# A graph network's second layer: the first group of a round prepared ahead of the node chunk, an index copy behind it, and activation tables loaded ahead of waits

## What is computed

```python
# layer 0
h = x @ W;  e = leaky_relu(a_src[src] + a_dst[dst], 0.2)
alpha = softmax of e over the edges of one dst
x = layernorm(x + tanh(segment_sum(h[src] * alpha[:, None], dst) + bias))
# layer 1
h = gelu(x @ W_pre + b_pre)
aggr = segment_sum(h[src] * edge_attr, dst)
v = x + aggr
y = gelu(gelu(v @ W1 + b1) @ W2 + b2)
out = layernorm(x + (v + y))
```

## Time and profile before

| what | value |
|---|---|
| median of 3 runs | 3843.77 us (3841.44 to 6046.89) |
| the profiled execution, time | 3842.3 us |
| the profiled execution, span from first to last instruction | 3840.5 us |
| busy share of the span: PE, DVE, ACT, POOL | 64%, 64%, 33%, 73% |
| mean granted TensorE clock | 0.701 of full speed |
| PE clock by tenths of full speed, 40 slices | `7555555555555555555558999999999999989997` |
| the same for POOL's busy share | `7777777777777777777747777777776667667664` |

### The profile page before, as it was taken

How to read it: one execution, slowest core, us unless ns; L and a number is a source line. 1 busy time by engine, 2 the same in 40 slices (tenths; PEclk the granted TensorE clock), 3 DMA queues, 4 the chain that set the end, 5 groups by cost and what they waited for, 6 DMA issues and landing times.

```text
span 3840.5 us, 66559 instructions
## 1 busy us (share of the span) xinstructions
PE 2439.5 (64%) x16652; PEld 1975.8 (51%) x16653; DVE 2446.4 (64%) x6235; ACT 1261.5 (33%) x3762; POOL 2789.9 (73%) x2950
## 2 busy tenths in 40 slices
PE   5433343434344444444448998898898888888886
PEld 3333333333333333333336777676776676766665
DVE  7444444444566666666657777777777777777765
ACT  4433343434455555555542111111111111121112
POOL 7777777777777777777747777777776667667664
PEclk7555555555555555555558999999999999989997
DMA  5222222222222222222224344344343333334332
GB/s 97 43 42 42 42 43 42 43 42 43 44 43 43 43 43 42 45 43 43 45 49 113 88 97 94 90 94 93 88 92 87 87 88 87 86 82 91 86 83 58
DMA packets 351534, 254.21 MB, mean 66 GB/s; under 512 B 254081, under 2 KB 279122, under 8 KB 351291
## 3 DMA queue, kind: packets, MB, share of 16 engines
q0 software_dynamic: 94016, 146.16, 19.6%
q1 hardware_dynamic: 241880, 99.40, 11.2%
q10 hardware_dynamic: 15394, 6.42, 0.6%
HBM read 244.43 MB, written 7.25 MB: 66 GB/s over the span
## 4 chain that ended last, share of the span: by engine, by line
POOL 34%; PE 28%; issue 17%; DVE 9%; ACT 7%; ACTq 2%; DMA 1%; DVEq 1%; POOLq 0%; SPq 0%
POOL rows L654 34%; PE bank L960 20%; PE bank L947 5%; ACT onehot L706 3%; DVE hot L1311 2%; DVE node L1327 1%; DVE score L1210 1%; ACT pair L726 1%; PE bank L969 1%; ACTq L699 1%; DMA rows<-table,src_i 1%; PE bank L933 1%; ACT L793 1%; ACT L800 0%; DMA src_i<-in_src_dram 0%
## 5 line engine op out<-in xcount | busy, mean ns | idle before, releaser
L654 POOL DMA_INDIRECT rows<-table,src_i x2850 | 2697.6, 947 | 999.0 <-issue 863.3
L960 PE MATMUL bank<-node,hot 128*128 128x288 bf16 x9310 | 1255.2, 298 | 27.5 <-issue 16.3
L897 PE MATMUL bank<-onehot,rows 128*97 128x72 f32 (+1 forms) x3056 | 586.2, 369 | 813.0 <-ACT onehot L736 813.0
L960 PEld LDWEIGHTS bank<-node,hot 128*128 128x128 bf16 x9310 | 946.9, 103 | 297.0 <-issue 19.1
L1311 DVE TENSOR_SCALAR hot<-node,key 128x642 bf16<-128x642 int16 x1862 | 870.5, 538 | 271.7 <-PE bank L960 233.8
L897 PEld LDWEIGHTS bank<-onehot,rows 128*97 128x97 f32 x3056 | 532.1, 281 | 852.3 <-issue 787.4
L947 PE MATMUL bank<-onehot,rows 128*96 128x72 f32 (+1 forms) x3136 | 327.1, 266 | 132.6 <-DVE acc L1356 132.5
L947 PEld LDWEIGHTS bank<-onehot,rows 128*96 128x96 f32 x3136 | 314.8, 179 | 154.0 <-DVE acc L1356 119.8
L706 ACT ACTIVATE onehot<-iota,far_dst 128x72 f32 (+1 forms) x1568 | 385.3, 328 | 23.3 <-ACT far_dst L703 0.7
L1189 DVE SCALAR_TENSOR_TENSOR other<-onehot,bank 128x576 f32<-128x576 f32 (+1 forms) x196 | 121.9, 622 | 390.0 <-ACT bank L719 321.6
L806 ACT ACTIVATE pair<-dst_i 128x8 f32<-128x8 int32 x196 | 35.3, 180 | 983.2 <-DVE rows L1345 966.5
(11 more groups left out here) (171 smaller groups left out, 2010.9 us busy)
## 6 DMA issues: line engine op xcount, KB each, us to landing
attr<-in_edge_attr_dram SPq DMA_DIRECT2D x190, 336.0 KB
rows<-table,src_i POOLq DMA_INDIRECT x2850
node<-in_src_dram SPq DMA_DIRECT2D x195, 64.0 KB
attr<-in_edge_attr_dram SPq DMA_DIRECT2D x190, 48.0 KB
dst_i<-in_dst_dram SPq DMA_DIRECT2D x200, 4.0 KB
src_i<-in_src_dram SPq DMA_DIRECT2D x195, 4.0 KB, 2.3
src_i<-in_src_dram SPq DMA_DIRECT2D x190, 3.5 KB
dst_i<-in_dst_dram SPq DMA_DIRECT2D x190, 3.5 KB
```

The lines of the kernel that those rows point to most:

```text
L654: pool.indirect_dma_start(rows[:, u, j * width:(j + 1) * width], None, table, bass.IndirectOffsetOnAxis(ap=src_i[:, u, j:j + 1], axis=0))\
L897: last = pe.matmul(total[:, 0:w], rows0(u, it)[:, j, 0:D1], wide(weights, w)[:, j, :], start=j == 0, stop=j == TILES - 1)
L960: last = pe.matmul(p_got[t], hot[:, c % HOTS, i, t * P:(t + 1) * P], tab[:, a, :, :].rearrange("p k d -> p (k d)"), start=a == 0, stop=a = ...
```

## The change

In layer 1, on DVE, `message` of a round's fifth group now also makes the mask (`marked`) and the seven gathered tiles' products (`multiplied`) of the next round's first group, ahead of the chunk. In the first group itself `added` comes first, then the marks of piece 0, the first reduction, the product of the fetched tile, which raises `e1_msg`, and only then the other four reductions. On ACT `shorten_src` moves behind the chunk. PE starts a chunk on `f_var` of the chunk before, where it waited for DVE to arrive (`f_go`); ahead of the very last chunk it waits for the last addition. In both layers ACT runs a one-element activation of the function that comes next ahead of the wait, so that its table is loaded by then; after each round of layer 0 it does so for Exp.

```diff
+            def table_for(f, k):
+                act.activation(unused[:, k:k + 1], zeros[0:1, 0:1], f)
+
             def middle(c, blocks=MB):
+                table_for(ACT.Tanh, 0)
...
-            groups(act, weights, lambda it: due(act, it, middle), alone=2)
+
+            def middle_due(it):
+                due(act, it, middle)
+                table_for(ACT.Exp, 3)
+            groups(act, weights, middle_due, alone=2)
             rest(act, middle)
 
             def final(c, blocks=MB):
+                table_for(ACT.Gelu, 2)
...
+                table_for(ACT.Sqrt, 1)
                 act.wait_ge(f_st, 16 * (c + 1))
-                act.wait_ge(f_var, c + 1)
+                act.wait_ge(f_var, c + 2)
...
-                if u == SLOTS - 1 and fetching(it):
+
+            def final_due(it):
+                due(act, it, final)
+                if fetching(it):
                     shorten_src(it + 1)
...
             def final(c, blocks=MB):
-                pe.wait_ge(f_go, c + 1)
+                pe.wait_ge(f_var, c + 1)
...
+            def marked(g, it, u, lo, w):
+                v.wait_ge(e1_fed, g + 1)
+                v.tensor_tensor(wide(onehot[:, u, :], w), over_window(p_dst1, w),
+                                over_tiles(iota[:, bass.ds(lo, w)], w), ALU.is_equal).then_inc(e1_hot, 1)
+
+            def multiplied(it, u, tiles):
+                v.wait_ge(e1.rows[u], gathered1(it, u))
+                return v.tensor_tensor(rows[:, u, 0:tiles * D], rows[:, u, 0:tiles * D], p_attr[:, 0:tiles * D], ALU.mult)
+
+            def multiplied_fetched(it, u):
+                v.wait_ge(g_out, it * 2 + (u > 0))
+                at = slice((TILES - 1) * D, TILES * D)
+                return v.tensor_tensor(rows[:, u, at], got[:, u, :], p_attr[:, at], ALU.mult)
+
+            def added(g, prev, w):
+                v.wait_ge(e1.acc, g + 1)
+                here = bass.ds(prev, w)
+                v.tensor_tensor(acc[0:D, here], acc[0:D, here], p_acc1[:, 0:w], ALU.add).then_inc(e1.free, 1)
...
                 if booked(it, u) and u == 0:
+                    added(g, prev, w)
+                    if fetching(it):
+                        marks(it, 0)
                     taken(it, range(1))
-                    v.wait_ge(g_out, it * 2)
-                    v.tensor_tensor(rows[:, u, cut:TILES * D], got[:, u, :], p_attr[:, cut:TILES * D], ALU.mult)\
-                        .then_inc(e1_msg, 1)
+                    multiplied_fetched(it, u).then_inc(e1_msg, 1)
                     taken(it, range(1, BOOKED))
                 else:
-                    product.then_inc(e1_msg, 1)
-                v.wait_ge(e1.acc, g + 1)
-                here = bass.ds(prev, w)
-                v.tensor_tensor(acc[0:D, here], acc[0:D, here], p_acc1[:, 0:w], ALU.add).then_inc(e1.free, 1)
+                    marked(g, it, u, lo, w)
+                    if booked(it, u):
+                        multiplied_fetched(it, u)
+                    multiplied(it, u, TILES - booked(it, u)).then_inc(e1_msg, 1)
+                    added(g, prev, w)
...
+                if u == SLOTS - 1 and it is not ROUNDS - 1:
+                    next_reg = v.alloc_register("next_" + named(it, u, ws))
+                    v.reg_alu(next_reg, after, (1 << BITS) - 1, ALU.bitwise_and)
+                    marked(g + 1, it + 1, 0, v.snap(next_reg, min_val=0, max_val=N - 1), ws[1])
+                    multiplied(it + 1, 0, TILES - 1)
```

More of the change, by code:

```diff
@@ L261, in gnn @@
         m_v = sem("m_v")
-        f_go = sem("f_go")
         f_y1 = sem("f_y1")
@@ L834, in _ @@
             feed(0, 0, 0)
-            groups(act, ahead, lambda it: due(act, it, final), alone=1)
+            groups(act, ahead, final_due, alone=1)
             rest(act, final)
@@ L994, in _ @@
             groups(pe, gather_sum, alone=1)
+            pe.wait_ge(e1.free, GROUPS + SLOTS)
             rest(pe, final)
@@ L1301, in _ @@
             v.sem_inc(g_out, 1)
+            v.sem_inc(f_var, 1)
             v.tensor_copy(key[:, :], key_i[:, :])
@@ L1332, in message @@
                 lo, further, prev = window(u, "1_" + named(it, u, ws))
[L1333 to L1343, removed]
-                v.wait_ge(e1.rows[u], gathered1(it, u))
-                product = v.tensor_tensor(rows[:, u, 0:cut], rows[:, u, 0:cut], p_attr[:, 0:cut], ALU.mult)
                 if booked(it, u) and u == 0:
+                    added(g, prev, w)
+                    if fetching(it):
+                        marks(it, 0)
                     taken(it, range(1))
-                    v.wait_ge(g_out, it * 2)
-                    v.tensor_tensor(rows[:, u, cut:TILES * D], got[:, u, :], p_attr[:, cut:TILES * D], ALU.mult)\
-                        .then_inc(e1_msg, 1)
+                    multiplied_fetched(it, u).then_inc(e1_msg, 1)
                     taken(it, range(1, BOOKED))
                 else:
-                    product.then_inc(e1_msg, 1)
-                v.wait_ge(e1.acc, g + 1)
-                here = bass.ds(prev, w)
-                v.tensor_tensor(acc[0:D, here], acc[0:D, here], p_acc1[:, 0:w], ALU.add).then_inc(e1.free, 1)
+                    marked(g, it, u, lo, w)
[3 more added lines that the diff above has]
+                    added(g, prev, w)
                 after = None if g is LAST else load_window(g + 1)
@@ L1382, in final @@
                 st = Steps(v, f_v, c * 7, 7)
-                v.sem_inc(f_go, 1)
                 v.wait_ge(f_g2, c + 1)
```

1 line of the change is left out of this document (added).

## The result

The changed kernel takes 3743.92 us (median of 4 runs, 3742.97 to 3744.58) where the kernel before takes 3844.1, a ratio of 0.9741 (0.9722 to 0.9761). That is faster by 2.6%. The forecast was 3754.8 and the range 3745 to 3786, so the direction is right, but the forecast is 10.9 us too high and the time lies 1.1 us under the range. The profiled execution took 3744.58 us with a span of 3742.7, 97.8 less than before.

What follows compares the result with a forecast made beforehand. POOL was taken to bound the kernel until 2758 us in layer 1, PE and DVE after that; 3840.5 us of span less 87.7 of POOL idle time and 1.3 for the last chunk, plus 3.3, gave 3754.8 us, range 3745 to 3786.

Steps and rivals of the forecast that it cites:

- The bound: Layer 1: POOL sets the pace up to 2758 us, then PE and DVE (the consumer); gain capped at POOL's 87.7 us idle.
- The round without a chunk: Layer 1, head of round: PE's window sum starts 1.6 us earlier, fuller clock adds up to 2.7; 3.6 us gain taken.
- The round with a chunk: Layer 1: Gelu 2.3 us earlier, window sum 5.0 earlier, at most 8.1 with the clock; 6.5 us gain taken.
- Both together: Consumer's gain over 29 rounds of layer 1: 15 x 6.5 + 14 x 3.6 = 148 us, bounds 97 and 182.
- rival 3: Layer 1, ahead of the chunk: DVE's products wait for their gather, holding up the chunk; +33 us, about 3876; chance 0.03.
- Rival 4: POOL's gathers slow beside DVE's denser marks; 1% longer each would be 17 us, 3772 us; chance 0.03.
- Rivals 1 and 2: Layer 1: consumer still binds in part, 3784 us, chance 0.2; wait just moves to piece 0's fetch, about 3810, chance 0.06.
- the sum: Whole kernel: span 3840.5 - 87.7 - 1.3 = 3751.5 us, plus 3.3 to the median, giving 3754.8 us.
- 94.0 - 21 x 0.3 = 87.7 us is real idle time: POOL in late layer 1: 21 waits for `src_i`, 94.0 us, less an ordinary gap each, leave 87.7 us to win.
- Layer 0: Table loads ahead of waits lie behind POOL; only the last two chunks can show, -2.6 to +0.8 us, taken as 0.
- The median of the runs is 3.3 us above this profile's span: Whole kernel: 3.3 us added to the forecast span of 3751.5 us to get the forecast run time of 3754.8.
- The tail: Last chunk, after all gathers: saves one table load, 1.3 us.

Runs made afterwards that it cites:

- six_after_3: The changed kernel with POOL making six gathers per booked group of layer 1, not seven, so part of the messages is missing: 3645.35 us, ratio 0.9505.
- products_behind: The changed kernel with the next round's first-group products back behind the chunk, only the mask ahead: ratio 0.9548, on a chip where the kernel before takes 5675 to 5805 us.
- l0_tables_3: The kernel before with only layer 0's part of the change, the one-element ACT activations that load tables early: 3837.74 us, ratio 0.9986.
- l1_only_2: The kernel before with only layer 1's part, all of the change but layer 0's four activation lines: 3746.98 us, ratio 0.977.
- add_late_3: The changed kernel with the addition moved back behind the reductions, as it stood before: 3771.9 us, ratio 0.9835.

## Why the prediction was right, and where it was not

The mechanism was right, and the sizes that went into the last sum were not. The step that failed is "3840.5 - 87.7 - 1.3 = 3751.5 us of span" with 3.3 us put on top: POOL's idle time was 92.6 us and not 87.7 (layer 1 won 91.6), layer 0 was put at nothing and the span got 4.95 us shorter there, and 1.2 us and not 3.3 lie between the span and the median.

**The bound.** POOL's pace against the consumer's, the change of hands at 2758 us, and the cap at POOL's idle time all held: idle time went from 92.6 us to nothing, and `six_after_3` shows the consumer beyond the cap.

**The round without a chunk.** 0.8 us was forecast for PE's gap, 0.91 is in the row, and the fetch behind it ran at full clock (60 products in 7.51 us). **The round with a chunk.** Gelu 0.05 behind PE, 0.04 measured; marks late by 0.4 and the last gap 1.3, measured 0.4 and 1.21. The gain of 5.0 us from chunk to window sum is not in this row (20.6 - 17.7 = 2.9), because the consumer waits for POOL there; in `six_after_3`, where it does not, the same stretch takes 15.8 us in the mean of 15 chunks against 20.4 before, 4.6 less. **Both together.** Taken were gains of 6.5 and 3.6 us a round, 148 in 29 rounds; `six_after_3` shows 6.7 and 3.5, 148.4 in the same rounds. That it fits to half a microsecond is luck, since the bounds were 97 and 182 and the clock's part was guessed within them.

**The wait of rival 3** is there: DVE waits for gathers 39.3 us in 19 waits between 2758 and 3600, and nine of them, 26.9 us with the longest 3.8, stand ahead of a chunk. POOL never stops meanwhile, so it costs no time here, as was argued; the kernel without this wait (`products_behind`) did not run at this pace. **Rival 4** did not come: layer 1's gathers took 0.7 ns more in the mean, 947.2 against 946.5, which is 1.0 us in all and not 17. Rivals 1 and 2 would have left POOL idle, and it is not.

**What failed** is the sum, by 3754.8 - 3743.9 = 10.9 us. Four terms, read from the two profiles:

1. "94.0 - 21 x 0.3 = 87.7 us is real idle time" counted only the gaps whose releaser is `src_i`. Four others in the same stretch of the kernel before bear the label of an ordinary gap:

```profile
2951.63 0.94 POOL L654 DMA_INDIRECT rows<-table,src_i  x1 [1.43 <-issue]
...
3074.02 0.94 POOL L654 DMA_INDIRECT rows<-table,src_i  x1 [1.51 <-issue]
...
3569.48 0.94 POOL L654 DMA_INDIRECT rows<-table,src_i  x1 [1.50 <-issue]
...
3701.63 0.94 POOL L654 DMA_INDIRECT rows<-table,src_i  x1 [1.77 <-issue]
```

They hold 6.21 - 4 x 0.3 = 5.0 us. The earlier trace rows showed the hint, a longest "issue" wait of 1.8 us where the earlier trace rows has 0.3, and it was passed over. With them the idle time is 92.6 us, layer 1 won 91.6 (slower single gathers took 1.0 back), and the term was 3.9 us short.

2. Layer 0: "between -2.6 and +0.8 us. I take 0". Measured is -2.8 for the part that `l0_tables_3` confirms. The bound was right within 0.2. The choice within it was wrong, and no reason was given for it: the last chunks do show in the time, each by some 1 us. Another 2.15 us came from an earlier last gather, which the runs do not tie to the change.

3. "The median of the runs is 3.3 us above this profile's span": the profiled execution's own time is 1.8 us above its span before (3842.3) and 1.9 after, and this is the part that carries over. The rest, 1.5 us, was that profile's luck. The kernel before varies: 3832.3 to 3848.4 in nine runs on one chip. The two profiles without layer 1's part have 92.6 and 82.2 us of POOL's idle time, so its stops are the likely source. At POOL's pace that is gone: 3742.97 to 3744.58 in four runs, 3645.17 and 3645.53, 3746.65 and 3747.31 in two. With the median after 1.2 above the profile's span, 2.1 us of the miss are here.

4. The tail was forecast at -1.3 and measured at -1.2.

3.9 + 4.95 + 2.1 - 0.1 = 10.85. No term is sure to better than some 3 us: layer 1 of `l1_only_2`, with the same gathers and no stops, is 2.6 us shorter than that of the changed kernel. The range's low end, 3745, left 10 us for all of this without working any of it out. With -2.6 for layer 0 and 5.0 for the mislabelled gaps, the first its own bound and the second in the trace it read from, the forecast would have been 3747.2, and the same 10 us below it would have held the time.

## What to carry to other kernels

Where one engine works at a constant pace and the others only let it down at times, the gain of any change to those others is that engine's idle time: take it as the span between its first and last instruction less count times period, not as the sum of the waits that a view labels. When a change removes a wait at the head of a loop, put first what frees another engine's buffer and what the next engine needs, and let the rest run beneath it. And if the next engine is only 3% faster than the one that binds, as here, relieving the one that binds is soon capped in its turn: of the 237 us that six gathers took off POOL 98.6 were won.

## What the hardware showed beyond this

**Chips on which engines stand without a wait.** The kernel before took 5675 to 5805 us on five chips, one of which gave the usual 3842.82 in a later batch, so it is no fixed property of a chip. POOL's gather is as long as ever (945 ns) there. The waits of the changed kernel on such a chip, 2900 to 5300 us:

```profile
DVE hot L1328 <- remote: 614.5, 74, 15.3
...
PEld bank L975 <- issue: 397.5, 437, 2.7
...
PEld bank L962 <- issue: 323.7, 267, 12.6
```

and PE in the middle of one fetch, which at the usual pace is 60 products in one piece:

```profile
4017.99 0.28 PE L975 MATMUL bank<-node,hot 128*128 128x288 bf16 x1 [0.44 <-issue]
...
4019.40 0.28 PE L975 MATMUL bank<-node,hot 128*128 128x288 bf16 x1 [1.13 <-issue]
4020.12 0.28 PE L975 MATMUL bank<-node,hot 128*128 128x288 bf16 x1 [0.44 <-issue]
```

The engine waits for nothing that the trace shows, and DVE and SP stand at the same time. That instructions come late is how I read it; the cause was not found. The kernel before had one such run too, 6046.89 us.

**Gathers beside VectorE.** In the first round of layer 1, where DVE splits the table with products of tiles that lie in SBUF, single gathers take 1.1 to 2.3 us, not 0.94, in all six profiles of the usual pace. Of the changed kernel:

```profile
2023.11 1.98 POOL L654 DMA_INDIRECT rows<-table,src_i  x1 [0.30 <-issue]
2025.39 0.94 POOL L654 DMA_INDIRECT rows<-table,src_i  x1 [0.30 <-issue]
...
2029.13 1.38 POOL L654 DMA_INDIRECT rows<-table,src_i  x1 [0.30 <-issue]
```

DVE's L1335, a tensor_tensor that reads both inputs from SBUF, runs from 2023.52 to 2024.27 and from 2028.95 to 2029.69, and L1338, another one, from 2022.85 to 2023.60. Both slow gathers began while one of these was running, and end 0.82 us after L1335 does. So do all 37 gathers over 1 us of these first 60 us of layer 1 in the six profiles: each ends 0.81 to 0.82 us after the last such tensor_tensor beside it, and 36 of them began while one was running. Of the gathers that began first and had a tensor_tensor start beside them, one grew (2.29 us, in `add_late_3`) and 55 took 0.94 to 0.96 us. By these traces it counts which of the two starts first. Beside the marks (tensor_scalar, L1328, from 2024.18 and 2030.08) the gathers keep it too: 888 of the changed kernel's gathers in layer 1 ran beside marks and took 0.948 us in the mean. The Trainium skill (SBUF — State Buffer, Who interferes with whom) says that a VectorE instruction with two SBUF inputs contends with a GpSimd instruction that reads SBUF, and infers that making a transfer's descriptors is spared by it. The trace fits the first, and the 1.26 us and more speak against the second. The prediction had feared the marks, and they do nothing that shows. All gathers over 1 us together cost 2 to 5 us of layer 1. No run changed the order of the two engines alone.
